# Local attention layers: q and k turned in two row tiles of 64 rows, and turns, mix and scores set together at the end of a step

## The reference, cut to what matters

```python
for i in range(DEPTH):                      # DEPTH = 6, HEADS = 16, DIM_HEAD = 64, WINDOW = 32
    x = attn_layer(shift_tokens(x), Wqkv[i], q_scale[i], k_scale[i], Wo[i]) + x
    x = ffn_layer(shift_tokens(x), ln_g[i], ln_b[i], W1[i], b1[i], W2[i], b2[i]) + x
# attn_layer: q, k, v = x @ Wqkv; q, k = l2norm * scale, then rotary with position scales
#   local attention: a window of 32 queries sees its own and the window before; softmax; out @ Wo
# ffn_layer: layernorm, W1 to 2 x 341, a * gelu(gate), W2
```

## Time and profile before

| | |
|---|---|
| median of 3 runs | 3350.36 us (3348.82 to 3352.47) |
| span of the profiled execution | 3349.9 us, 0.5 us under the median |
| busy share of that span: PE, PEld | 97%, 61% |
| busy share: DVE, POOL, ACT | 88%, 79%, 71% |
| DMA share of 16 engines, queue 1 | 31.9% |

### The profile page before, as it was taken

One profiled execution on the slowest core, in us unless ns is written; L12 is line 12 of the kernel. 1 busy time (PEld: TensorE's weight loads), 2 busy tenths in 40 slices (PEclk: granted clock), 3 DMA queues, 4 the chain that ended last, 5 costly groups with the idle time before them and its releaser, 6 DMA issues. The chain is left out here.

```text
span 3349.9 us, 130995 instructions
## 1 busy us (share of the span) xinstructions
PE 3240.1 (97%) x56388; PEld 2053.0 (61%) x56388; DVE 2944.3 (88%) x3353; ACT 2374.4 (71%) x4288; POOL 2640.7 (79%) x1408
## 2 busy tenths in 40 slices
PE   8988999999999999999999999999999999998997
PEld 4555666666666666666666666666666666654554
DVE  6889989999898989999999989898999989975888
ACT  6875677767777677777677767777776777766886
POOL 1229988888888888888888888888888888873667
PEclk9999999999999999999999999999999999999998
DMA  2002433433433443334333334433343343340000
GB/s 96 2 2 65 125 112 109 129 118 114 121 109 116 128 122 116 115 109 129 119 115 119 109 116 126 124 116 111 113 128 118 113 122 109 115 147 26 2 11 18
DMA packets 229205, 336.06 MB, mean 100 GB/s; under 512 B 39062, under 2 KB 151060, under 8 KB 228244
## 3 DMA queue, kind: packets, MB, share of 16 engines
q1 hardware_dynamic: 228628, 327.68, 31.9%
HBM read 124.14 MB, written 102.76 MB: 68 GB/s over the span
## 5 line engine op out<-in xcount | busy, mean ns | idle before, releaser
L828 PE MATMUL psum<-w_qkv,f_xs 128*128 128x512 f32 x2304 | 1078.2, 604 | 11.1 <-DVE f_times_sin L1243 9.5
L1426 POOL TENSOR_TENSOR f_rotated<-f_times_cos,f_times_sin 128x1024 f32<-128x1024 f32 x384 | 909.5, 2369 | 4.2 <-DVE f_times_sin L1243 4.1
L1434 POOL TENSOR_TENSOR f_rotated<-f_rotated,f_rnorm 128x1024 f32<-128x1024 f32 x384 | 723.5, 1905 | 30.3 <-POOL f_rotated L1426 2.2
L828 PEld LDWEIGHTS psum<-w_qkv,f_xs 128*128 128x128 f32 x2304 | 408.7, 191 | 394.0 <-issue 370.3
L1050 ACT ACTIVATE f_squares<-psum 128x1024 f32<-128x1024 f32 x384 | 393.4, 1025 | 338.0 <-PE psum L828 337.1
L1418 POOL TENSOR_TENSOR f_probs<-f_probs,f_rowsum 128x1024 f32<-128x1024 f32 x192 | 365.8, 1905 | 312.9 <-DVE f_rowsum L1284 312.9
L1242 DVE TENSOR_TENSOR f_times_cos<-psum,rot 128x1024 f32<-128x1024 f32 x384 | 469.7, 1223 | 120.1 <-ACT f_squares L1050 115.9
L1070 ACT COPY f_qkT<-psum 128x1024 f32<-128x1024 f32 x384 | 369.7, 1013 | 208.4 <-PE psum L838 208.4
L1243 DVE TENSOR_TENSOR f_times_sin<-psum,rot 128x1024 f32<-128x1024 f32 x384 | 466.1, 1214 | 0.0
L1250 DVE TENSOR_REDUCE f_sumsq<-f_squares 128x16 f32<-128x1024 f32 x384 | 463.5, 1209 | 0.0
L838 PEld LDWEIGHTS psum<-consts,f_rotated 128*128 128x128 f32 x3072 | 349.4, 141 | 89.6 <-issue 79.8
(11 more groups left out here) (178 smaller groups left out, 5166.9 us busy)
## 6 DMA issues: line engine op xcount, KB each, us to landing
f_v_moved<-f_v SPq DMA_DIRECT2D x768, 128.0 KB, 2.8
turned_blocks<-w_qkv SPq DMA_DIRECT2D x192, 512.0 KB, 3.0
f_probsT<-turned_blocks SPq DMA_DIRECT2D x768, 128.0 KB, 2.8
w_qkv<-in_l_wqkv SPq DMA_DIRECT2D x18, 512.0 KB, 4.1
w_o<-in_l_wo SPq DMA_DIRECT2D x6, 512.0 KB, 4.5
w_qkv<-in_ctxT SPq DMA_DIRECT2D x1, 2048.0 KB, 8.7
w<-in_l_w SPq DMA_DIRECT2D x6, 341.0 KB
out<-x_f_result SPq DMA_DIRECT2D x7, 256.0 KB, 2.2
```

The lines of the kernel that those rows point to most:

```text
L828: mm = pe.matmul(pairs[i][:, j * BANK:(j + 1) * BANK], xs[g % 2][:, u % GB, :], w_qkv[:, part * INNER + j * BANK:part * INNER + (j + 1) * ...
L1426: pool.tensor_tensor(rotated[u % 2][:, part].rearrange("p h (s d) -> p s h d", s=2), halves(times_cos[part][:, :]), halves(times_sin[part] ...
L1434: pool.tensor_tensor(rt, rt, rnorm[u % 2][:, part * H:(part + 1) * H].unsqueeze(2).broadcast_to([P, H, HD]), ALU.mult).then_inc(normalised ...
```

## The change

Three things change in the local layers. (1) A turn of 128 rows x 128 columns against a 128x128 identity becomes two of 64 rows x 128 columns against a 64x64 identity, one on the upper and one on the lower half of the array's rows, into the two banks of the pair. Each part issues 16 transposes with 64 moving columns instead of 8 with 128. (2) `copy_qk` reads the pair in the order that follows from it; the copied data and their size are the same. (3) Every engine's loop has a new order: on TensorE turns, mix and scores close the step, as k turned, mix, q turned, scores; the mix has lag 5 instead of 6, the masking, maxima, lowering, exponentials, sums and normalisation of a unit all lag 3; ROTATING and END follow. SP's loop is as it was.

```diff
-            ROTATING = (("q", 0, 1), ("up2", 13, GB), ("mix", 6, 1), ("k", 0, 1), ("v", 4, 1), ("scores", 2, 1), ("out", 6, 2),
+            ROTATING = (("up2", 13, GB), ("variance", 10, GB), ("q", 0, 1), ("k", 0, 1), ("up0", 11, GB), ("v", 4, 1),
...
                     for t in range(IT):
-                        tr = pe.transpose(pairs[i][:, t * S:(t + 1) * S],
-                                          rotated[u % 2][:, part, 2 * t:2 * t + 2, :].rearrange("p h d -> p (h d)"), ident)
+                        for j in range(2):
+                            rows = slice(HROWS * j, HROWS * j + HROWS)
+                            tr = pe.transpose(pairs[i][:, j * BANK + t * HROWS:j * BANK + (t + 1) * HROWS],
+                                              rotated[u % 2][rows, part, 2 * t:2 * t + 2, :].rearrange("p h d -> p (h d)"),
+                                              ident[rows, rows], tile_position=(rows.start, 0))
                     tr.then_inc(turned[part], 1)
...
-                    act.copy(qkT[u % 2][:, part].rearrange("p t n -> p (t n)"), pair(("qT", "kT")[part], u)).then_inc(copied[part], 1)
+                    act.copy(qkT[u % 2][:, part].rearrange("p t (j n) -> p j t n", j=2),
+                             pair(("qT", "kT")[part], u).rearrange("p (j t n) -> p j t n", j=2, t=IT)).then_inc(copied[part], 1)
```

More of the change, by code:

```diff
@@ L47 @@
 HALFV = INNER // 2
+HROWS = P // 2
 CONSTS = 2 * P + NEAR + 4 * HD + 4
@@ L678, in local_layers @@
             NG_ALL = UNITS // GB
-            ROTATING = (("q", 0, 1), ("up2", 13, GB), ("mix", 6, 1), ("k", 0, 1), ("v", 4, 1), ("scores", 2, 1), ("out", 6, 2),
-                        ("up0", 11, GB), ("mean", 7, GB), ("up1", 11, GB), ("variance", 10, GB), ("down", 13, GB), ("kT", 1, 1),
-                        ("qT", 1, 1))
+            ROTATING = (("up2", 13, GB), ("variance", 10, GB), ("q", 0, 1), ("k", 0, 1), ("up0", 11, GB), ("v", 4, 1),
+                        ("up1", 11, GB), ("out", 6, 2), ("down", 13, GB), ("mean", 7, GB), ("kT", 1, 1), ("mix", 5, 1),
+                        ("qT", 1, 1), ("scores", 2, 1))
             pair_of, turn = {}, 0
@@ L688, in local_layers @@
                         turn += 1
-            END = (("up2", 44), ("mix", 186), ("v", 188), ("scores", 190), ("down", 44), ("kT", 191), ("qT", 191), ("v", 189),
-                   ("scores", 191), ("mix", 187), ("v", 190), ("out", 93), ("variance", 45), ("v", 191), ("mean", 46), ("mix", 188),
-                   ("mix", 189), ("variance", 46), ("up0", 45), ("up1", 45), ("up2", 45), ("mix", 190), ("mix", 191), ("down", 45),
+            END = (("up2", 44), ("v", 188), ("scores", 190), ("down", 44), ("kT", 191), ("qT", 191), ("v", 189), ("scores", 191),
+                   ("mix", 187), ("v", 190), ("out", 93), ("variance", 45), ("v", 191), ("mean", 46), ("mix", 188), ("mix", 189),
+                   ("variance", 46), ("up0", 45), ("up1", 45), ("up2", 45), ("mix", 190), ("mix", 191), ("down", 45),
                    ("out", 94), ("out", 95))
@@ L949, in pe @@
                 for step in range(2, UNITS):
+                    mlp_up(step - 13, 2)
+                    mlp_variance(step - 10)
                     project(step, 0)
-                    mlp_up(step - 13, 2)
-                    mix(step - 6)
                     project(step, 1)
+                    mlp_up(step - 11, 0)
                     project(step - 4, 2)
-                    scores(step - 2)
[L956 to L963, removed]
+                    mlp_up(step - 11, 1)
+                    project_out(step - 6)
+                    mlp_down(step - 13)
+                    mlp_mean(step - 7)
+                    transpose_qk(step - 1, 1)
+                    mix(step - 5)
+                    transpose_qk(step - 1, 0)
+                    scores(step - 2)
                 mlp_up(179, 2)
-                mix(186)
                 project(188, 2)
@@ L1153, in act @@
                 for step in range(2, UNITS):
-                    square(step, 0)
+                    mlp_square(step - 9)
+                    copy_mix(step - 6)
                     reciprocal_norms(step - 1)
@@ L1171, in act @@
                 reciprocal_norms(191)
-                exponentials(188)
                 mlp_gelu(179, 2)
@@ L1344, in dve @@
                         start_layer(step // NB)
+                    turn_probs(step - 5)
+                    mask_scores(step - 3)
+                    row_maxima(step - 3)
+                    mlp_hidden(step - 13, 2)
                     products(step, 0)
-                    turn_probs(step - 5)
-                    mlp_hidden(step - 13, 2)
                     products(step, 1)
-                    mask_scores(step - 2)
+                    mlp_hidden(step - 11, 0)
+                    sum_squares(step, 1)
+                    add_down(step - 13)
                     sum_squares(step, 0)
+                    mlp_hidden(step - 11, 1)
                     mlp_centre(step - 7)
                     add_out(step - 6)
[L1353 to L1357, removed]
+                    row_sums(step - 3)
                     clamp_norms(step)
-                    row_maxima(step - 2)
+                mask_scores(189)
+                row_maxima(189)
                 turn_probs(187)
-                row_sums(188)
                 mlp_hidden(179, 2)
@@ L1455, in pool @@
                     rotate(step - 1, 1)
+                    lower(step - 3)
                     normalise(step - 1, 1)
                     normalise(step - 1, 0)
-                    lower(step - 3)
                     rotate(step, 0)
                     mlp_scale(step - 10)
-                    normalise_probs(step - 4)
+                    normalise_probs(step - 3)
                 rotate(191, 1)
@@ L1464, in pool @@
                 normalise(191, 0)
-                normalise_probs(188)
                 lower(189)
```

13 lines of the change are left out of this document (6 added, 7 removed).

## The result

The changed kernel takes 3541.78 us (median of 5 runs, 3536.95 to 3556.22), the kernel before 3350.36 (5 runs, 3342.08 to 3356.09). The ratio is 1.0577, with a 95% interval of 1.0553 to 1.0601: 5.8% slower, where 3225 us was predicted. The profiled execution of the changed kernel took 3556.22 us, its span is 3554.4.

What follows compares the result with a forecast made beforehand. TensorE's instruction stream was taken as the bound; 180 steps each gaining 0.72 us (turns 0.51, borders 0.21) give 130, lateness costs 5: 3350.4 - 130 + 5 = 3225 us. Range 3190 to 3300, the forecast's own 3208 to 3255.

Steps and rivals of the forecast that it cites:

- part 2: TensorE's order: tiled stages closing the step enter and leave the array once, borders gaining 0.21 of 0.72 us per step.
- The bound is TensorE's instruction stream: Whole kernel: TensorE busy 97% of the span, steps of 14.39 us, 1.3 us margin before DVE would be the bound.
- Part 1, the turns: Turns of k and q on TensorE: eight rounds of two transposes, 0.62 us per turn, gaining 0.51 us per step.
- The rival of ordinary loads: Turns on TensorE: loads as slow as ordinary ones, each turn 1.04 us, 3377 us in all, slower; chance 0.12.
- the forecast's rows: TensorE's stage times: two turns 1.75 us before, 0.62 each after; going into tiles 0.10, coming back 0.11.
- The cheap-borders rival: Borders inside the tiled stretch on TensorE cost nothing, 0.10 us less at each of three, 3190 us; chance 0.10.
- Part 3, the other engines: DVE, POOL, ACT, SP: same work fits a 13.67 us step; probabilities have 1.1 us slack; lateness adds 5 us.
- once or twice per layer: Sign in the profile after: the mix waits for the fetched probabilities no more often than this.
- Wrong it would be through: Signs against the forecast: TensorE waits naming DVE, POOL or DMA above 20 us, or granted clock below 1.00 in layers.
- The prediction's rival: TensorE's granted clock falls in the now longer tiled stretch, ending on the slower side; chance 0.02.
- the forecast's 13.67: Average step in us over 800 to 2800, TensorE above 99% busy, against 14.39 before.

Runs made afterwards that it cites:

- mix mended (e9): Kernel before with row-tiled turns, the mix right behind them, its copy earlier on ACT and the probabilities' turn earlier on DVE: 3318.95 us, ratio 0.9908.
- turns alone: Kernel before with the row-tiled turns and the matching `copy_qk`, old order on every engine: 3284.12 us, ratio 0.9811.
- filler: Changed kernel with two unused whole-array products of 512 columns added per step between q's turn and the scores: 3636.72 us, ratio 1.0847.
- half the scores: Changed kernel with every second head pair's scores left out and each remaining product covering all 128 keys, so another output: 3286.24 us, ratio 0.9809.
- order alone: Kernel before with the changed kernel's order on every engine and the old whole-array turns: 3472.45 us, ratio 1.0383.
- v between, mended: Changed kernel with v projected between q's turn and scores, `prepare` behind ACT's copies, v's store behind that of the probabilities on SP: 3491.98 us, ratio 1.0416.
- mix after turns: Kernel before with row-tiled turns and the mix moved first in the loop, right behind the turns, scores apart: 3842.93 us, ratio 1.1476.
- v between: Changed kernel with v's projection moved from mid-step to between q's turn and the scores, ACT's copies moved to match: 4099.04 us, ratio 1.2255.
- scores thrice: Kernel before with its scores issued three times over the same place, 768 instructions in a row: 5110.34 us in one run.

## Why the prediction was wrong

**The step that failed** is the sum of part 2, "0.10 + 0.62 + 1.54 + 0.62 + 1.41 + 0.11 = 4.40 us against 5.12", together with "The bound is TensorE's instruction stream": each stage was taken at the time it has among slow products, and putting them in a row was costed at nothing but borders. No term stood for the delivery of the instructions themselves. It is 1.42 us per step (184.6 us over 130 steps). The border of whole-array and tiled products, 0.21 us, was counted as a pure cost; that the slow products between the tiled stages also gave the delivery its time had no place in the sum.

**Part 1, the turns: right.** 0.64 us measured, 0.62 forecast; loads 139 ns, as the 140 in the earlier trace rows had it. The rival of ordinary loads (1.04) is refuted. The Trainium skill, page TensorE: Matmul & The Clock Gate, section LDWEIGHTS (loading the stationary operand), puts a load at its columns over 1.2 GHz, an estimated 0.85 us for eight rounds of these loads; the 0.64 measured does not bear it out for such transposes. Alone, the turns gain 3347.0 - 3284.1 = 63 us, 0.35 per step; by the forecast's rows it would be 0.61 less one more entry and return, 0.21, so 0.40.

**Part 2, the borders: right in size.** Mix 1.53, turns 0.64, each with its border in it. The cheap-borders rival is refuted.

**Part 3, the other engines: right in the changed kernel.** The probabilities landed a median of 3.0 us before their mix, and no row of TensorE's waits names DVE, POOL or DMA with 20 us. In six of 130 steps the mix started within 0.3 us of their landing, at most some 12.8 us in all (its rows under "issue"); the prediction allowed for that once or twice per layer. With steps of 15.38 this was no test of a step of 13.67, in which 1.7 us less would be at hand.

**The clock.** "Wrong it would be through ... a granted clock below 1.00 in the layers": so it came. In the layers it was at the lower level for 112.6 us in 23 stretches (3.4 in one before). At half speed that is an estimated 56 us lost, if TensorE was at whole-array products all that time. The prediction's rival put a fall down to the longer tiled stretch, and gave it 0.02; across these runs the lower level goes with standing still, for whatever reason (idle of TensorE over 800 to 2800; the lower level from 300 us to the last turn; where waits for data prevail the first column has no count; "mix mended (e9)" is `e9_mix_after_turns_mended`):

```
kernel                supply standstill per step   TensorE idle   lower level
before                0.01 us                        7.4 us           3.4 us
turns alone           0                              8.5             13.7
mix mended (e9)       -                             33.4             17.1
filler                0.22                          34.0             34.1
half the scores       0.42                          69.1             23.9
order alone           0.49                          75.5             17.1
v between, mended     0.35                         124.5             92.2
after                 1.42                         166.3            112.6
mix after turns       -                            285.0            274.5
v between             -                            331.2            669.0
scores thrice         5.27                         395.5            986.5
```

In the two rows above "scores thrice" TensorE waits mostly for data, not for its instructions. The order of the upper rows is not that of their idle time, so the clock's part is shown only in the large.

**The account.** Per step, over the forecast's 13.67: 1.42 standstill, 56 / 180 = 0.31 clock, 0.04 turns, 15.44 in all against 15.38 measured. 180 steps of 1.71 more are 308 of the 317 us by which the forecast missed.

The Trainium skill, page Runtime: NRT & Kernel Launch, section Instruction fetch mechanics, holds that the next block of 256 instructions is fetched while the current one runs, and that this stays hidden, since an engine dispatches more slowly than blocks arrive. The block size agrees with the trace (253 matmuls and loads to a packet, some records being missing). That it stays hidden holds for the kernel before (1.1 us of standstill in 2000), not for 512 instructions in 4.2 us, 8 ns each. I had not weighed that rule; it would have spoken for the forecast.

**Open:** what makes a packet start when it does. Against TensorE's stop its start lies between 1.9 us before and 0.2 after, but for a few, and why it is early in some steps is not settled; nor is how much further ahead it could be. Over 800 to 2800 no two packets start less than about 3.3 us apart in any of these kernels, while the end of a changed step would use one in 2.1 us (4.2 us for 512 instructions); whether that distance is a limit of its own or follows from the 2.4 us of a delivery no run here tells.

## What to carry to other kernels

Small tiled products are quick on the array and still each an instruction: count how many stand in a row, divide by the time they take, and compare with the instruction queue's packets in the trace (here 256 instructions to a packet, and some 2.4 us from its start until TensorE goes on) before gathering tiled stages into one block. Slow whole-array products that have to be done anyway, 0.43 us each for two instructions, buy that time when they stand between them, for 0.21 us of borders; the best kernel here takes the new turns and leaves the order alone, 3284 us, 1.9% under before. The sign is an idle row with the releaser "issue" in the middle of a stage, about once per step, that ends 1.2 to 1.5 us after a packet of the instruction queue. The name alone is not enough: before the mix the same row stood for probabilities that had not landed (215.2 us with v between).

## What the runs showed of the hardware that was not expected

- Small products and loads, 5.5 ns each in the scores (1.41 / 256) and 8.0 in the mix (1.53 / 192), outrun their own delivery: in a long row 256 of them take 4.0 us, of which 2.1 us are idle.
- The delivery was not overlapped in the kernel with the scores thrice: its packets start about when TensorE stops (median 0.1 us after), last about 1.0 us, and TensorE goes on some 1.4 us after their end.
- Kernels in which TensorE stands still more run longer at the lower level of its granted clock: 112.6 us with stops of mostly 1 to 2.5 us once per step (an estimated 56 us lost), 986.5 us in the kernel with the scores thrice.
- Two row tiles of fp32 transposes with 64 moving columns run side by side: 16 take 0.64 us, so the two that do the work of one whole-array transpose take 0.08, where that one took 0.109.
